# A ring of eight weight columns, and the low part of new expert weights ahead of the low part of the rows, in a mixture-of-experts stage

## Chip, core and metric

The kernel runs on one NeuronCore of a Trainium2 chip. The metric is the device time of one execution in microseconds (us). Its engines are TensorE (PE in the profile, PEld its weight loads), VectorE (DVE), ScalarE (ACT), GpSimd (POOL) and SyncE (SP). Each takes its instructions in order from a sequencer of its own, which also does the register work, the branches and the waits (a q behind the engine's name); semaphores order the engines among each other.

## The reference

Two residual layers on x of 4 x 2048 x 512 floats: a small selective state space model, and then a mixture of 64 experts, which is the part in question:

```python
swb = sigmoid(einsum('bsd,de->bse', x, w_router)) + b_router
...                                    # 4 of 8 groups, then 8 of 64 experts for each token
topk_w = 2.5 * topk_w / sum(topk_w)
sort = argsort(idx_flat); tok = sort // 8; x_sorted = x_flat[tok]
g = ragged_dot(x_sorted, we_gate, group_sizes)      # 512 -> 256, of each row's expert
u = ragged_dot(x_sorted, we_up, group_sizes)        # 512 -> 256
o = ragged_dot(silu(g) * u, we_down, group_sizes)   # 256 -> 512
y = zeros.at[tok].add(o * w_sorted[:, None])
```

There are 8192 tokens with 8 experts each, and a shared expert besides, which an earlier stage does.

## The kernel before

Earlier stages normalize, scan the states, route the tokens and write a table: 576 tiles of 128 rows, each of one expert. The last stage, `expert_tiles`, goes through that table; it is all that the change touches. One word of the table (`Words`, read by `value_load` at L1301) holds a tile's expert, the slot of its weights, and whether the expert is new, so that its weights have to be made. 64 of the tiles are such.

fp32 products are made of rounded parts: a factor's high part is its cast to float32r, its low part the difference to it; a product is high times high, high times low, and low times high. So each step has these pieces, i being the tile:

- `turn_x(i)` (TensorE, L1407): four transposes of the gathered rows into `ps_x`, the one buffer that there is of it.
- `keep_x(i)` (ScalarE): the high part of `ps_x` (`xT_high`, L1524), then the row numbers (L1526) and the column of routing weights (`weight`, L1528).
- `keep_low(i)` (VectorE, L1587): the low part of `ps_x` (`xT_low`). Only after it may `ps_x` be written again: `turn_x(i + 1)` waits for `xT_low_ready`.
- `split_high(i, part)` (ScalarE, L1516) and `split_low(i, part)` (VectorE, L1579): the high and low part of a new expert's weights, part 0 for gate and up (128 x 2048), part 1 for down (128 x 1024). For other tiles the engine only looks at the word, branches past, drains and counts the semaphore up ("the look").
- `gate_up(i)` (TensorE, L1437): twelve matmuls, eight with `xT_high`, four with `xT_low`. It waits for `w_low_ready[0]`, which `split_low(i, 0)` counts up. Between its matmuls TensorE's sequencer reads ahead words of the table (`read_ahead`): up to three, by the tile's place in a cycle of eight; in tiles that are multiples of eight one more stands ahead of it (L1487).
- `activate` (ScalarE, silu, L1535), `hidden` (VectorE, product, L1599), `turn_h`, `keep_h`, `keep_h_low`, `down` (TensorE, L1456), and `scale(i)` (VectorE, L1606): output rows times `weight`, in `y`. GpSimd adds them to the output and gathers rows ahead.
- Every four tiles VectorE marks (`mark`, L1611) and picks (`pick`, L1618 to L1627) which rows belong to tiles to come, and TensorE searches between (`find`, L1419): mark in VectorE's steps with i%4 = 2, find in TensorE's with i%4 = 3.

The orders are written by hand in each engine's `step(i, s)`. TensorE: `turn_x(i + 1)`, `find` in every fourth step, `gate_up(i)`, `turn_h(i - 1)`, `down(i - 2)`. VectorE: `keep_low(i + 1)`, `split_low(i + 1, 0)`, `split_low(i, 1)`, pick or mark, `hidden(i)`, `keep_h_low(i - 1)`, `scale(i - 2)`. ScalarE: row numbers, `keep_x(i + 1)`, `split_high(i + 2, 0)`, `split_high(i + 1, 1)`, `activate(i)`, `keep_h(i - 1)`. So a new tile n has the first half of its weights made low in VectorE's step n - 1, while TensorE works on tile n - 1, and the second half in step n. `weight` has four columns; `keep_x(i)` writes one of them after `scale(i - 4)` has read it.

Of the kernel before, what the change touches and what calls it, by code (L numbers as in the profile page):

```python
# [5 lines left out]
ALU = mybir.AluOpType  # L6
# [8 lines left out]
P = 128  # L15
# [18 lines left out]
UNROLL, SHORT = 8, 4  # L34
# [7 lines left out]
def after(eng, sem, count):  # L42

    if not isinstance(count, int) or count > 0:
        eng.wait_ge(sem, count)
# [1152 lines left out]
def expert_tiles(nc, k):  # L1198
# [8 lines left out]
    with ExitStack() as ctx:  # L1207
        def sb(name, shape, dt=F32):
            return ctx.enter_context(nc.sbuf_tensor("e_" + name, shape, dt))
# [12 lines left out]
        x_ids = sb("x_ids", [P, UNROLL], U32)  # L1222
        y_ids = sb("y_ids", [P, UNROLL], U32)
        x = sb("x", [P, XS, ROW])
        weight = sb("weight", [P, SHORT])
        xT_high = sb("xT_high", [P, 2, DC, P], F32R)
        xT_low = sb("xT_low", [P, 2, DC, P], F32R)
        silu = sb("silu", [P, 2, F])
# [41 lines left out]
        y_made = sem("y_made")  # L1270
# [26 lines left out]
        def exists(i):  # L1297
            return not isinstance(i, int) or 0 <= i < TILES
# [206 lines left out]
        @block.scalar  # L1505
        def _(act):
            words = Words(act)

            def split_high(i, s, part):
                if part == 0:  # L1510
                    act.wait_ge(w_loaded[s % WS], 48 // WS * (i - s % WS) + 48)
                    after(act, gu_done, i - WSLOTS + 1)
                else:
                    after(act, y_done, i - WSLOTS + 1)
                act.sem_inc(act_begun, 1)
                split_weights(act, words, s, lambda half, place: nc.scalar.copy(  # L1516
                    w_high[:, bass.ds(place, 1), PARTS[part]], w_raw[:, bass.ds(half, 1), PARTS[part]]))
                act.drain().then_inc(w_high_ready[part], 1)  # L1518

            def keep_x(i, s, slot):  # L1520
                e = act.snap(words.expert(s), min_val=0, max_val=E - 1)
                act.wait_ge(xt_done, i + 1)
                after(act, gu_done, i - 1)
                nc.scalar.copy(xT_high[:, s % 2], ps_x[:]).then_inc(xT_high_ready, 1)  # L1524
                after(act, retired, i - YS + 2)
                nc.scalar.copy(y_ids[:, bass.ds(slot, 1)], tile_ids[:, bass.ds(i, 1)])  # L1526
                after(act, y_made, i - SHORT + 1)
                nc.scalar.copy(weight[:, s % SHORT:s % SHORT + 1],  # L1528
                               x[:, bass.ds(slot, 1), bass.ds(e + D, 1)].rearrange("p o d -> p (o d)")) \
                    .then_inc(weight_ready, 1)  # L1530

            def activate(i, s):
                act.wait_ge(gu_done, i + 1)
                after(act, h_made, i - 1)
                nc.scalar.activation(silu[:, s % 2, :], ps_gu[s % 2][:, 0, :], ACT.Silu).then_inc(silu_ready, 1)  # L1535

            def keep_h(i, s):
                act.wait_ge(ht_done, i + 1)
                after(act, y_done, i - 1)
                nc.scalar.copy(hT_high[:, s % 2], ps_h[:]).then_inc(hT_high_ready, 1)  # L1540

            def take_ids(i, column):
                act.wait_ge(picked, i + 1)
                nc.scalar.copy(x_ids[:, bass.ds(column, 1)], tile_ids[:, bass.ds(i, 1)]).then_inc(ids_ready, 1)  # L1544

            def step(i, s, slot):
                if s == 0:
                    words.load(i + 1, s + 1)
                words.load(i + 2, (s + 2) % SHORT)
                if exists(i + AHEAD_IDS):  # L1550
                    take_ids(i + AHEAD_IDS, slot(AHEAD_IDS))
                if exists(i + 1):
                    keep_x(i + 1, (s + 1) % SHORT, slot(1))
                if exists(i + 2):
                    split_high(i + 2, (s + 2) % SHORT, 0)
                if exists(i + 1):
                    split_high(i + 1, (s + 1) % SHORT, 1)
                activate(i, s)
                if exists(i - 1):
                    keep_h(i - 1, (s - 1) % SHORT)  # L1560

            for i in range(AHEAD_IDS):
                take_ids(i, i)
            for i in range(2):
                words.load(i, i)
                split_high(i, i, 0)
            split_high(0, 0, 1)
            keep_x(0, 0, 0)
            short_walk(act, step)
            keep_h(TILES - 1, SHORT - 1)  # L1570

        @block.vector
        def _(v):
            words = Words(v)

            def split_low(i, s, part):
                v.wait_ge(w_high_ready[part], i + 1)
                v.sem_inc(dve_begun, 1)
                split_weights(v, words, s, lambda half, place: nc.vector.tensor_tensor(  # L1579
                    w_low[:, bass.ds(place, 1), PARTS[part]], w_raw[:, bass.ds(half, 1), PARTS[part]],  # L1580
                    w_high[:, bass.ds(place, 1), PARTS[part]].bitcast(F32), ALU.subtract))
                v.drain().then_inc(w_low_ready[part], 1)

            def keep_low(i, s):
                v.wait_ge(xT_high_ready, i + 1)
                after(v, gu_done, i - 1)
                nc.vector.tensor_tensor(xT_low[:, s % 2], ps_x[:], xT_high[:, s % 2].bitcast(F32),  # L1587
                                        ALU.subtract).then_inc(xT_low_ready, 1)
# [13 lines left out]
            def scale(i, s, slot):  # L1602
                v.wait_ge(y_done, i + 1)
                v.wait_ge(weight_ready, i + 1)
                after(v, retired, i - YS + 2)
                nc.vector.tensor_scalar(y[:, bass.ds(slot, 1), :].rearrange("p o d -> p (o d)"), ps_y[s % 2][:],  # L1606
                                        weight[:, s % SHORT:s % SHORT + 1], None, ALU.mult).then_inc(y_made, 1)

            def mark(i):

# [19 lines left out]
            def step(i, s, slot):  # L1630
                if s == 0:
                    words.load(i, s)
                words.load(i + 1, (s + 1) % SHORT)
                if exists(i + 1):
                    keep_low(i + 1, (s + 1) % SHORT)
                    split_low(i + 1, (s + 1) % SHORT, 0)
                split_low(i, s, 1)
                if s == 1 and exists(i - s - SHORT + AHEAD_FIND):
                    pick(i - s - SHORT + AHEAD_FIND, 2)
                if s == 2 and exists(i - s + AHEAD_FIND):  # L1640
                    mark(i - s + AHEAD_FIND)
                if s == 3 and exists(i - s + AHEAD_FIND):
                    pick(i - s + AHEAD_FIND, 0)
                hidden(i, s)
                if exists(i - 1):
                    keep_h_low(i - 1, (s - 1) % SHORT)
                if exists(i - 2):
                    scale(i - 2, (s - 2) % SHORT, slot(UNROLL - 2))
# [100 lines left out]
```

## Time and profile before

| | before |
|---|---|
| median of 3 runs (lowest to highest) | 3974.49 us (3974.14 to 3979.03) |
| the profiled execution | 3973.47 us, span 3971.7 us |
| busy: TensorE, VectorE, ScalarE, GpSimd | 92%, 58%, 34%, 40% of the span |
| granted TensorE clock, mean | 0.971 of full speed |

`expert_tiles` is the part from about 900 us to the end. The timeline lists instructions by start in us from the start of the span, with their duration, engine, line, operation, tiles, how many were merged, and in brackets how long the engine had been idle before, and what ended it. TensorE's ends are modelled, and its instructions overlap. Steps are therefore measured from start to start.

### The profile page before, as it was taken

How to read it: one execution, taken by the hardware profiler on the slowest of the kernel's cores; microseconds unless marked ns; L12 is line 12 of the kernel's file. 1: busy time of each engine (PE TensorE's matmuls, PEld its weight loads, DVE VectorE, ACT ScalarE, POOL GpSimd, SP SyncE). 2: the span in 40 equal slices, each digit the busy share in tenths (PEclk: the TensorE clock that was granted, in tenths of full speed). 3: DMA queues.
4: the chain of work that ended last, by engine and by line, in shares of the span. 5: the costliest groups of instructions: out<-in, count | busy, mean ns of one | idle time of the engine just before them, and what ended most of it. 6: DMA issues, size and time to landing. Idle time of an engine off the chain costs nothing.

```text
span 3971.7 us, 110141 instructions
## 1 busy us (share of the span) xinstructions
PE 3650.4 (92%) x16856; PEld 2774.8 (70%) x16857; DVE 2313.6 (58%) x5802; ACT 1349.9 (34%) x4031; POOL 1602.0 (40%) x1208
## 2 busy tenths in 40 slices
PE   6809999967999999999999999999999999999996
PEld 3404445536877777787778778787888777787785
DVE  5364555555666665656665565656555666666653
ACT  2212222213333433434333343334333343334331
POOL 1010000004555555555555455555555555455443
PEclk9959999988999999999999999999999999999998
DMA  3322323225666676667666666666666676666654
GB/s 113 106 61 86 98 97 98 96 56 122 125 154 149 153 155 122 149 127 167 141 134 127 158 137 124 138 139 152 124 127 140 122 169 153 140 133 154 137 102 74
DMA packets 216177, 502.40 MB, mean 126 GB/s; under 512 B 46587, under 2 KB 46715, under 8 KB 215360
## 3 DMA queue, kind: packets, MB, share of 16 engines
q0 software_dynamic: 129024, 320.94, 43.4%
q1 hardware_dynamic: 86592, 177.77, 13.6%
q10 hardware_dynamic: 512, 3.15, 0.3%
q8 instruction: 17, 0.28, 0.0%
q14 instruction: 32, 0.26, 0.0%
HBM read 1115.65 MB, written 191.41 MB: 329 GB/s over the span
## 4 chain that ended last, share of the span: by engine, by line
PE 59%; DVE 5%; issue 5%; DVEq 2%; ACT 2%; DMA 2%; ACTq 1%; POOLq 0%; POOL 0%; SPq 0%
PE e_ps_gu L1437 34%; PE e_ps_y L1456 16%; PE e_ps_x L1407 5%; DVE e_w_low L1579 3%; PE e_ps_h L1466 3%; ACT e_w_high L1516 2%; DMA out<-e_y,e_y_ids 2%; PE e_ps_find L1419 1%; DVEq L1301 1%; ACTq L1301 1%; DVE e_past L1611 1%; DVE e_y L1606 1%; DVE e_below L1622 0%; DVEq L1579 0%; ACT e_silu L1535 0%
## 5 line engine op out<-in xcount | busy, mean ns | idle before, releaser
L1381 POOL DMA_INDIRECT out<-e_y,e_y_ids x576 | 935.9, 1625 | 1326.5 <-ACT e_weight L1528 582.4
L1373 POOL DMA_INDIRECT e_x<-token_rows,e_x_ids x576 | 615.9, 1069 | 273.5 <-issue 172.7
L1437 PE MATMUL e_ps_gu<-e_w_high,e_xT_high 128*128 x2304 | 688.4, 419 | 15.1 <-issue 5.1
L1437 PE MATMUL e_ps_gu<-e_w_low,e_xT_high 128*128 x2304 | 646.6, 399 | 6.4 <-issue 4.8
L1437 PE MATMUL e_ps_gu<-e_w_high,e_xT_low 128*128 x2304 | 650.4, 401 | 0.2 <-issue 0.2
L1606 DVE TENSOR_SCALAR e_y<-e_ps_y,e_weight 128x512 f32 (+1 forms) x576 | 430.9, 748 | 243.6 <-PE e_ps_y L1456 202.9
L1587 DVE TENSOR_TENSOR e_xT_low<-e_ps_x,e_xT_high 128x512 fp32r<-128x512 f32 x576 | 397.7, 690 | 286.9 <-ACT e_xT_high L1524 173.6
L1437 PEld LDWEIGHTS e_ps_gu<-e_w_high,e_xT_low 128*128 128x128 f32 x2304 | 428.8, 189 | 128.1 <-issue 29.2
L1437 PEld LDWEIGHTS e_ps_gu<-e_w_low,e_xT_high 128*128 128x128 f32 x2304 | 428.8, 188 | 126.5 <-issue 31.1
L1535 ACT ACTIVATE e_silu<-e_ps_gu 128x256 f32<-128x256 f32 x576 | 221.2, 384 | 821.5 <-PE e_ps_gu L1437 627.0
L1437 PEld LDWEIGHTS e_ps_gu<-e_w_high,e_xT_high 128*128 128x128 f32 x2304 | 396.2, 191 | 98.1 <-issue 37.3
L1524 ACT CAST e_xT_high<-e_ps_x 128x512 fp32r<-128x512 f32 x576 | 336.5, 584 | 294.1 <-PE e_ps_x L1407 289.2
L1456 PE MATMUL e_ps_y<-e_w_high,e_hT_high 128*128 x1152 | 411.6, 438 | 0.0
L1407 PEld LDWEIGHTS e_ps_x<-ident,e_x 128*128 128x128 f32 x2304 | 366.5, 204 | 57.2 <-issue 6.5
L1599 DVE TENSOR_TENSOR e_h<-e_silu,e_ps_gu 128x256 f32<-128x256 f32 x576 | 241.6, 419 | 282.2 <-ACT e_silu L1535 259.8
L1407 PE MATMUL e_ps_x<-ident,e_x 128*128 128x128 f32 x2304 | 365.7, 281 | 7.8 <-DVE e_xT_low L1587 6.8
L1456 PE MATMUL e_ps_y<-e_w_high,e_hT_low 128*128 x1152 | 362.5, 396 | 0.0
L1456 PE MATMUL e_ps_y<-e_w_low,e_hT_high 128*128 x1152 | 362.5, 396 | 0.0
L1544 ACT CAST e_x_ids<-e_tile_ids (+1 forms) x576 | 110.1, 192 | 503.6 <-issue 403.5
L1466 PEld LDWEIGHTS e_ps_h<-ident,e_h 128*128 128x128 f32 x1152 | 226.4, 197 | 51.7 <-DVE e_h L1599 3.4
L1456 PEld LDWEIGHTS e_ps_y<-e_w_high,e_hT_low 128*128 128x128 f32 x1152 | 218.2, 189 | 51.1
L1579 DVE TENSOR_TENSOR e_w_low<-e_w_raw,e_w_high x128 | 225.4, 1761 | 48.7 <-ACTq L1518 25.0
(245 smaller groups left out, 3926.0 us busy)
## 6 DMA issues: line engine op xcount, KB each, us to landing
e_w_raw<-in_L_ffn_we_gate SPq DMA_DIRECT2D x576, 512.0 KB
e_w_raw<-in_L_ffn_we_up SPq DMA_DIRECT2D x576, 512.0 KB
e_w_raw<-in_L_ffn_we_down SPq DMA_DIRECT2D x576, 512.0 KB
a_x<-in_L_attn_x SPq DMA_DIRECT2D x64, 256.0 KB, 3.4
t_x_in<-in_L_attn_x SPq DMA_DIRECT2D x64, 256.0 KB, 2.8
token_rows<-t_xn SPq DMA_DIRECT2D x64, 256.0 KB, 3.1
out<-t_y_out SPq DMA_DIRECT2D x64, 256.0 KB, 2.0
e_x<-token_rows,e_x_ids POOLq DMA_INDIRECT x576
```

Source lines behind the costliest of these rows:

```text
L1373: pool.indirect_dma_start(x[:, s % XS, :], None, k.rows, bass.IndirectOffsetOnAxis(x_ids[:, s:s + 1], 0)) \
L1381: pool.indirect_dma_start(k.out, bass.IndirectOffsetOnAxis(y_ids[:, s:s + 1], 0), y[:, s % YS, :], None, compute_op=ALU.add).then_inc(adde ...
L1407: last = nc.tensor.transpose(ps_x[:, c, :], chunks[:, c, :], k.ident[:])
L1437: last = nc.tensor.matmul(ps_gu[s % 2][:], x[:, s % 2, c, :], w[:, c], start=(n == 0), stop=(n == 3 * DC - 1))
L1456: last = nc.tensor.matmul(ps_y[s % 2][:], x[:, s % 2, c, :], w[:, c], start=(n == 0), stop=(n == 3 * FC - 1))
L1466: last = nc.tensor.transpose(ps_h[:, c, :], chunks[:, c, :], k.ident[:])
L1524: nc.scalar.copy(xT_high[:, s % 2], ps_x[:]).then_inc(xT_high_ready, 1)
L1535: nc.scalar.activation(silu[:, s % 2, :], ps_gu[s % 2][:, 0, :], ACT.Silu).then_inc(silu_ready, 1)
L1579: split_weights(v, words, s, lambda half, place: nc.vector.tensor_tensor(w_low[:, bass.ds(place, 1), PARTS[part]], w_raw[:, bass.ds(half, ...
L1587: nc.vector.tensor_tensor(xT_low[:, s % 2], ps_x[:], xT_high[:, s % 2].bitcast(F32), ALU.subtract).then_inc(xT_low_ready, 1)
L1599: nc.vector.tensor_tensor(h[:, s % 2, :], silu[:, s % 2, :], ps_gu[s % 2][:, 1, :], ALU.mult).then_inc(h_made, 1)
L1606: nc.vector.tensor_scalar(y[:, bass.ds(slot, 1), :].rearrange("p o d -> p (o d)"), ps_y[s % 2][:], weight[:, s % SHORT:s % SHORT + 1], Non ...
```

## The change

The ring `weight` gets eight columns in place of four, so that `keep_x(i)` waits for `scale(i - 8)`; the column is found by a register in place of a constant. And VectorE does `split_low(i + 1, 0)` ahead of `keep_low(i + 1)`.

```diff
-        weight = sb("weight", [P, SHORT])
+        weight = sb("weight", [P, UNROLL])
...
-                after(act, y_made, i - SHORT + 1)
-                nc.scalar.copy(weight[:, s % SHORT:s % SHORT + 1],
+                after(act, y_made, i - UNROLL + 1)
+                nc.scalar.copy(weight[:, bass.ds(slot, 1)],
...
-                                        weight[:, s % SHORT:s % SHORT + 1], None, ALU.mult).then_inc(y_made, 1)
+                                        weight[:, bass.ds(slot, 1)], None, ALU.mult).then_inc(y_made, 1)
...
                 if exists(i + 1):
+                    split_low(i + 1, (s + 1) % SHORT, 0)
                     keep_low(i + 1, (s + 1) % SHORT)
-                    split_low(i + 1, (s + 1) % SHORT, 0)
                 split_low(i, s, 1)
```

What it moves stands in VectorE's order, here from the read of the table word to the branch for the down part, in the step with the mark. Names start with e_; "waits" are the semaphores that a row waits for. Before:

```order
L1301 TENSOR_LOAD tiles
L1301 ISA x2
L1585 REGISTER_ALU
L1587 TENSOR_TENSOR e_xT_low<-e_ps_x,e_xT_high 128x512 [waits e_gu_done,e_xT_high_ready]
L1328 REGISTER_ALU [waits e_w_high_ready0]
L1328 COMPARE_AND_BRANCH
L1579 REGISTER_ALU x2
L1579 ISA
L1579 REGISTER_ALU
L1579 TENSOR_TENSOR e_w_low<-e_w_raw,e_w_high 128x2048
L1328 UNCONDITIONAL_BRANCH
L1328 COMPARE_AND_BRANCH [waits e_w_high_ready1]
```

The same place in the changed kernel:

```order
L1301 TENSOR_LOAD tiles
L1301 ISA x2
L1577 REGISTER_ALU
L1328 REGISTER_ALU [waits e_w_high_ready0]
L1328 COMPARE_AND_BRANCH
L1579 REGISTER_ALU x2
L1579 ISA
L1579 REGISTER_ALU
L1579 TENSOR_TENSOR e_w_low<-e_w_raw,e_w_high 128x2048
L1328 UNCONDITIONAL_BRANCH
L1587 TENSOR_TENSOR e_xT_low<-e_ps_x,e_xT_high 128x512 [waits e_gu_done,e_xT_high_ready]
L1328 COMPARE_AND_BRANCH [waits e_w_high_ready1]
```

The low part of the rows (L1587) has moved behind the low part of the weights and behind the register work and branch ahead of that; the branch for the down part now follows it directly.

TensorE's order is the same in both kernels. This is where it waits for the two, behind the transposes of h of one step; the rows are the last ones of a step and the first ones of the next:

```order
L1466 MATMUL e_ps_h<-ident,e_h 128x128 [waits e_h_made]
L1466 MATMUL e_ps_h<-ident,e_h 128x128
L1407 MATMUL e_ps_x<-ident,e_x 128x128 [waits e_xT_low_ready,e_gathered3]
L1407 MATMUL e_ps_x<-ident,e_x 128x128 x3
L1437 REGISTER_ALU [waits e_h_made,e_xT_high_ready,e_w_low_ready0]
L1437 ISA
L1437 MATMUL e_ps_gu<-e_w_high,e_xT_high 128x512
```

The wait for the rows' low part stands ahead of the four transposes, the wait for the weights' low part behind them; both rows have kept their places.

## Rows read from the trace of the kernel before

**Rows 1.** Page, part 4: the chain that ended last, shares by line.
```profile
PE e_ps_gu L1437 34%; PE e_ps_y L1456 16%; PE e_ps_x L1407 5%; DVE e_w_low L1579 3%; PE e_ps_h L1466 3%; ACT e_w_high L1516 2%; DMA out<-e_y,e_y_ids 2%; PE e_ps_find L1419 1%; DVEq L1301 1%; ACTq L1301 1%; DVE e_past L1611 1%; DVE e_y L1606 1%; DVE e_below L1622 0%; DVEq L1579 0%; ACT e_silu L1535 0%
```

**Rows 2.** Timeline of TensorE, a step with no new expert.
```profile
2919.46 0.63 PE L1407 MATMUL e_ps_x<-ident,e_x 128*128 128x128 f32 x4
2919.85 1.17 PE L1437 MATMUL e_ps_gu<-e_w_high,e_xT_high 128*128 x4
...
2921.79 1.10 PE L1437 MATMUL e_ps_gu<-e_w_high,e_xT_low 128*128 x4
...
2924.37 0.63 PE L1407 MATMUL e_ps_x<-ident,e_x 128*128 128x128 f32 x4
```

**Rows 3.** Page, part 5: groups of VectorE; count, busy us, mean ns, idle before.
```profile
L1587 DVE TENSOR_TENSOR e_xT_low<-e_ps_x,e_xT_high 128x512 fp32r<-128x512 f32 x576 | 397.7, 690 | 286.9 <-ACT e_xT_high L1524 173.6
...
L1579 DVE TENSOR_TENSOR e_w_low<-e_w_raw,e_w_high x128 | 225.4, 1761 | 48.7 <-ACTq L1518 25.0
```

**Rows 4.** Timeline of VectorE in its step 384; tile 385 is new.
```profile
2932.26 0.69 DVE L1587 TENSOR_TENSOR e_xT_low<-e_ps_x,e_xT_high 128x512 fp32r<-128x512 f32 x1 [1.27 <-ACT e_xT_high L1524]
2932.93 2.29 DVE L1579 TENSOR_TENSOR e_w_low<-e_w_raw,e_w_high  x1
```

**Rows 5.** Timeline of TensorE, its step 385.
```profile
2934.73 0.63 PE L1407 MATMUL e_ps_x<-ident,e_x 128*128 128x128 f32 x4
2935.49 0.96 PE L1437 MATMUL e_ps_gu<-e_w_high,e_xT_high 128*128 x3
...
2938.33 1.31 PE L1437 MATMUL e_ps_gu<-e_w_high,e_xT_low 128*128 x4
...
2941.11 0.63 PE L1407 MATMUL e_ps_x<-ident,e_x 128*128 128x128 f32 x4
```

**Rows 6.** TensorE's sequencer in that time: duration ns min/median/max, first and last start.
```profile
L45 PEldq EVENT_SEMAPHORE  x1: 51/51/51, 2933.0 to 2933.0; - x1
...
L1437 PEldq ALU_OP  x1: 36/36/36, 2935.3 to 2935.3; - x1
...
L1301 PEldq TENSOR_LOAD <-tiles x3: 299/302/307, 2935.9 to 2938.0; - x3
```

**Rows 7.** Timeline of VectorE in its step 414; tile 414 is new.
```profile
3090.36 0.72 DVE L1611 TENSOR_TENSOR e_past<-slot_row,begin 64x512 bf16<-64x512 f32 x1 [0.21 <-issue]
```

**Rows 8.** Timeline of TensorE, the start of its step 415.
```profile
3090.18 0.63 PE L1407 MATMUL e_ps_x<-ident,e_x 128*128 128x128 f32 x4
3091.27 0.73 PE L1419 MATMUL e_ps_find<-ranks,e_past 64*128 x4 [0.45 <-DVE e_past L1611]
```

**Rows 9.** Timeline of ScalarE in its step 321; tile 323 is new.
```profile
2606.28 0.19 ACT L1528 COPY e_weight<-e_x 128x1 f32 x1 [0.34 <-DVE e_y L1606]
2606.80 1.91 ACT L1516 CAST e_w_high<-e_w_raw  x1 [0.32 <-issue]
```

**Rows 10.** Timeline of VectorE, from the end of its step 321 into 322.
```profile
2610.30 0.74 DVE L1606 TENSOR_SCALAR e_y<-e_ps_y,e_weight 128x512 f32 x1
2611.43 0.69 DVE L1587 TENSOR_TENSOR e_xT_low<-e_ps_x,e_xT_high 128x512 fp32r<-128x512 f32 x1 [0.39 <-ACT e_xT_high L1524]
2612.08 2.29 DVE L1579 TENSOR_TENSOR e_w_low<-e_w_raw,e_w_high  x1
2614.98 0.68 DVE L1611 TENSOR_TENSOR e_past<-slot_row,begin 64x512 bf16<-64x512 f32 x1 [0.61 <-issue]
```

**Rows 11.** Timeline of TensorE, in its step 323.
```profile
2615.86 0.72 PE L1419 MATMUL e_ps_find<-ranks,e_past 64*128 x4 [0.81 <-DVE e_past L1611]
```

**Rows 12.** Timeline of VectorE in its steps 239 and 240; tile 240 is new.
```profile
2166.83 2.31 DVE L1579 TENSOR_TENSOR e_w_low<-e_w_raw,e_w_high  x1
...
2173.41 0.69 DVE L1587 TENSOR_TENSOR e_xT_low<-e_ps_x,e_xT_high 128x512 fp32r<-128x512 f32 x1 [1.03 <-issue]
```

**Rows 13.** Waits: who, for whom; us in total, times, longest.
```profile
ACT e_weight L1528 <- DVE e_y L1606: 210.5, 237, 3.2
...
PE e_ps_x L1407 <- DVE e_xT_low L1587: 6.8, 3, 6.1
```

## The prediction

> **What bounds the kernel now.** I read the page's chain of work that ended last first: 55% of it is TensorE's gate/up, down and transposing matmuls (34 + 16 + 5), 3% VectorE's low part of new weights (L1579) [rows 1]. Then the timeline of TensorE where nothing new is loaded. From one block of four transposes (L1407) to the next a step takes 2924.37 - 2919.46 = 4.91 us; gate/up starts 0.39 after the transposes and lasts to 2921.79 + 1.10, 3.04 us [rows 2]. No row there has idle time ahead of it, so a plain step can gain nothing. What can be won or lost lies at new experts: L1579 has 128 instructions [rows 3], two per new expert, so 64 tiles bring new weights; the first opens the stage, 63 stand in it. For those I read VectorE's, ScalarE's and TensorE's timelines around one tile of each kind. The kind is the tile's place in VectorE's cycle of four steps, because the search work differs by step. Placing the 128 instructions among the 576 of L1587 gives 10 tiles n with n%4 = 1, 18 with 2, 17 with 3 and 18 with 0, of which 8 are multiples of 8.
>
> The reader is to see what ends TensorE's wait there. For tile 385 VectorE does keep_low at 2932.26 (0.69 long, done 2932.95) and then the low part, 2932.93 + 2.29 = 2935.22 [rows 4]. TensorE's transposes of the next tile start at 2934.73 with no wait, gate/up of 385 at 2935.49; the step is 2941.11 - 2934.73 = 6.38, 1.47 over a plain one [rows 5]. Little of this is the wait for the low part itself: gate/up lasts to 2938.33 + 1.31 = 2939.64, 4.15 us instead of 3.04. The sequencer's rows show why. It passes a wait (L45) at 2933.0, just as keep_low ends and 1.7 before those transposes run; it stands at gate/up until 2935.3, just after the low part; and only then reads three words of the tile table, from 2935.9 to 2938.0, in between issuing matmuls [rows 6]. So **TensorE's sequencer is held by keep_low ahead of the transposes and by the low part ahead of gate/up, and after the last release gate/up ends 2939.64 - 2935.22 = 4.42 us later.** At the transposes themselves TensorE hardly ever waits for keep_low today: 6.8 us in three times [rows 13].
>
> **The change, part by part.** *The swap.* It adds no data work: 64 low parts and 576 keep_lows stay. Before, keep_low came first and released the transposes while the low part ran. Now the low part comes first, so keep_low ends about 2.3 us later at every new expert, and TensorE's transposes, which stand ahead of gate/up in its program, wait for both in turn.
>
> Tile 385: the low part can start where keep_low did, 2932.26, plus the sequencer's look at the table word, the branch and the addresses, which was hidden under keep_low and took at most 0.67 (2932.93 - 2932.26). Bounds 2932.26 and 2932.93; I take 2932.75, near the upper, since VectorE was waiting on its sequencer there. It ends 2935.04. keep_low follows after a drain and two waits: between 0 and the 0.69 of a skipped part; I take 0.2, then 0.69: 2935.93. The transposes, at 2934.73 before, start at about 2936.0. The sequencer is released at 2935.98 instead of 2935.22, issues four transposes (0.2) and then has the same 4.42: gate/up ends at 2940.6 instead of 2939.64. **+1.0 us.** Nine tiles of this kind; the tenth, 257, follows two other new experts within three tiles, so that other waits may cover it, and I count it 0: **+9.0**.
>
> n%4 = 2 (tile 414): the same +1.0 in its own step, but the next step has the search, and that waits today: its transposes start at 3090.18, the search only at 3091.27, after the mark (L1611) at 3090.36 + 0.72 [rows 7, 8]. TensorE being 1.0 later at 3091.2 + 0.6 finds the mark about done. VectorE's own way to the mark hardly changes: in the step of the low part the look at the down part now hides under keep_low, but the look at the gate/up part comes bare. **+0.1, 18 tiles: +1.8**, bounds -0.2 and +0.5.
>
> n%4 = 3 (tile 323): here the mark is in the same step as the low part, and the search waits for it until 2615.86 [rows 10, 11]; the transposes are early in any case. VectorE waited for ScalarE before keep_low (0.39), and the low part started at 2612.08 [rows 10]. *The ring* acts here: ScalarE's copy of the weight column waited 0.34 for VectorE's scaling of four tiles back [rows 9], and behind it on ScalarE stand the 1.91 us high part of the new expert, the silu, and with it VectorE's product and scaling. Without that wait all of it moves up by about 0.35; in all, ScalarE gives 210.5 us to this wait [rows 13], nearly all of it where nothing hangs on it. With the swap the low part starts no sooner than the scaling's end (2610.30 + 0.74 = 2611.04) and no later than the look's 0.67 behind keep_low's old start (2612.10), both less 0.35; I take 2611.35, between the two, 0.7 earlier. keep_low (0.2 + 0.69) now stands between it and the mark, but hides some 0.55 of the 0.61 from the low part's end (2614.37) to the mark (2614.98). 0.7 - 0.9 + 0.55 = 0.35: **-0.35, 17 tiles: -6.0**, bounds 0 and -0.75.
>
> n%4 = 0 (tile 240): the low part ends at 2166.83 + 2.31 = 2169.14; half a us earlier with ring and swap, but then keep_low (0.2 + 0.69) follows, and the sequencer is released at 2169.55, 0.37 later than now [rows 12]. At multiples of 8 one more table word is read between transposes and gate/up (L1487), so far behind the wait's cover: bounds 0.3, a bare load, and 1.05, the spacing of the three [rows 6]; I take 0.7. With 0.2 for the transposes 1.27, of which I take 0.9, because the next step waits for a late keep_low today (1.03 idle ahead of it [rows 12]) and then no longer does: **8 tiles, +7.2**. The other 10 have slack in their own step (the step before has the search), but in the next keep_low comes some 0.3 later through the bare look: **+0.3, 10 tiles: +3.0**.
>
> *Elsewhere.* The ring's register column adds one register instruction to ScalarE; in plain steps both have idle time. In a plain step keep_low comes later by the look without new weights: between 0 and 0.67, I take 0.4. The tightest place is the one of tile 385's L45 row: the sequencer is released 1.7 ahead of the transposes, then 1.3. Issuing gate/up with its three words took from 2935.3 to 2938.0 and some 0.7 for the last word, 3.4 us for 3.04 of matmuls, so about 0.9 is left over, and I count 0. If that cover is gone it is the third rival.
>
> Sum: 9.0 + 1.8 - 6.0 + 7.2 + 3.0 = **+15.0 us**. The profiled execution took 3973.47; so 3988.5 there, and against the median of 3974.49, which is 1.0 above it, **3989**.
>
> [...] The sequencer's rows [rows 6] show it stopped at the wait ahead of the transposes until keep_low is done, as its next instruction, the one at gate/up, comes only after. [...]
>
> **The rivals.** (1) *The sequencer isn't held at the transposes.* Then it reads its words under the wait, gate/up follows the transposes by 0.39 and lasts 3.04 [rows 2]: tile 385 ends at 2939.4 (-0.2 x 10 = -2), 414 goes by the mark (-0.2 x 18 = -3.6), 323 as above (-6), and n%4 = 0 loses today's stall of the next step (about 0.5, half of its 1.03, x 18 = -9): -20.6, **3954**, faster. For it: every low part does come earlier. Against: the sequencer's rows [rows 6]. It decides if gate/up ends within 3.5 us of keep_low's end. Chance 0.15. (2) *Gains and losses cancel*: the look costs nothing on VectorE and tile 323's kind gains 0.75 (-13), while 385's loses 0.7 (+6) and the rest as above at half: within 8 us of **3974**. Chance 0.27. (3) *Plain steps lose too*: if that 0.9 isn't there, for table words that come slowly, 0.2 in each of some 138 steps with i%4 = 1 adds 28: **4017**. Against: the slack, and steps that run without idle time now [rows 2]. Chance 0.1. That the change doesn't do what it says, a swap without effect since VectorE's sequencer is the limit, is the lower bound of tile 385's shift and lies in (2).
>
> **How the numbers follow.** My forecast has 0.48, with its own range 3978 to 4002 from the bounds. A measurement of this kernel tells about 0.2%, 8 us, from no change. Faster: rival 1 and a part of 2, 0.18. Same: most of 2 and the low end of the forecast, 0.26. Slower: the rest, 0.56. The range 3956 to 4008 leaves out the far halves of 1 and 3.
>
> **What would show it.** Right: in the profile after, L1407 waits on e_xT_low L1587 about 1 us at the tiles with n%4 = 1 and 2, some 25 to 30 us in all, where now it is 6.8 [rows 13]; ScalarE's wait of e_weight on e_y is gone; the search's wait on e_past is smaller. Wrong: no wait at L1407, or gate/up after it in 3.05 us, or plain steps over 4.91.

## The result, and the profile after

| | before | changed |
|---|---|---|
| median of 4 runs each (lowest to highest) | 3976.28 us (3974.14 to 3979.03) | 4046.31 us (4041.55 to 4050.68) |
| ratio to before | | 1.0175, 95% interval 1.0158 to 1.0193 |
| span of the profiled execution | 3971.7 us | 4046.0 us |
| granted TensorE clock, mean | 0.971 | 0.969 |

The changed kernel is 70 us slower, where 15 was forecast and the third rival said 43. The chain that ended last has gained TensorE, VectorE's share of new weights (L1579) stays at 3% [rows 1]:

```profile
PE e_ps_gu L1437 37%; PE e_ps_y L1456 17%; PE e_ps_x L1407 6%; DVE e_w_low L1579 3%; PE e_ps_h L1466 3%; PE e_ps_find L1419 1%; DMA out<-e_y,e_y_ids 1%; ACT e_w_high L1516 1%; DVEq L1301 1%; DVE e_xT_low L1587 1%; DMA e_w_raw<-in_L_ffn_we_down 0%; DVEq L1579 0%; DVE e_past L1611 0%; ACTq L1301 0%; ACT e_silu L1535 0%
```

The waits that the prediction named have changed as it said; ScalarE's wait of `weight` for the scaling no longer stands in the list [rows 13]. In the changed kernel:

```profile
PE e_ps_x L1407 <- DVE e_xT_low L1587: 37.5, 34, 5.8
...
PE e_ps_find L1419 <- DVE e_past L1611: 8.5, 18, 2.7
```

The second of the two stood in the kernel before as

```profile
PE e_ps_find L1419 <- DVE e_past L1611: 29.5, 34, 2.7
```

At the transposes there are 37.5 us in 34 waits, where 25 to 30 were forecast and 6.8 in 3 stood before. So the waits at new experts came as expected; what they cost is told further down. Tile 385 once more, VectorE, then TensorE [rows 4, 5], then the L45 row of TensorE's sequencer, its next wait behind those transposes [rows 6]:

```profile
2988.99 2.29 DVE L1579 TENSOR_TENSOR e_w_low<-e_w_raw,e_w_high  x1 [1.83 <-issue]
2991.48 0.69 DVE L1587 TENSOR_TENSOR e_xT_low<-e_ps_x,e_xT_high 128x512 fp32r<-128x512 f32 x1 [0.20 <-issue]
```

```profile
2992.23 0.75 PE L1407 MATMUL e_ps_x<-ident,e_x 128*128 128x128 f32 x4 [1.19 <-DVE e_xT_low L1587]
...
2995.37 1.30 PE L1437 MATMUL e_ps_gu<-e_w_high,e_xT_low 128*128 x4
...
2998.14 0.63 PE L1407 MATMUL e_ps_x<-ident,e_x 128*128 128x128 f32 x4
```

```profile
L45 PEldq EVENT_SEMAPHORE  x1: 51/51/51, 2992.2 to 2992.2; - x1
```

keep_low starts 0.20 after the low part, as taken. The transposes wait 1.19 for it (1.27 forecast). The sequencer passes L45 at 2992.2, and gate/up ends at 2995.37 + 1.30 = 2996.67, 4.50 behind keep_low's end at 2992.17 (forecast: 2940.6 - 2935.93 = 4.67).

What was not forecast stands where nothing new is loaded. A step's length is taken from one block of transposes to the next. Of the 338 steps that are neither n - 1, n, n + 1 nor n + 2 of a new expert, those with i%4 = 1 rose from 4.91 to 5.37 (medians; 86 steps, +31.1 us in sum), those with i%8 = 2 from 4.91 to 5.09 (42 steps, +5.0); the medians of all others, sorted by i%8, kept their length to 0.01. Step 365 of the changed kernel, TensorE:

```profile
2886.09 0.63 PE L1407 MATMUL e_ps_x<-ident,e_x 128*128 128x128 f32 x4
2886.47 1.17 PE L1437 MATMUL e_ps_gu<-e_w_high,e_xT_high 128*128 x4
2887.48 1.34 PE L1437 MATMUL e_ps_gu<-e_w_low,e_xT_high 128*128 x4
2888.66 1.31 PE L1437 MATMUL e_ps_gu<-e_w_high,e_xT_low 128*128 x4
```

The blocks of four follow each other at 1.01 and 1.18 us, and the last two last 1.34 and 1.31 instead of 1.10 [rows 2]: TensorE is given its matmuls late. What stands behind that is told by the step ahead of it. In the kernel before, the timeline has the transposes that open step 364, GpSimd's add (L1381), and VectorE's keep_low:

```profile
2828.38 0.63 PE L1407 MATMUL e_ps_x<-ident,e_x 128*128 128x128 f32 x4
...
2830.42 1.59 POOL L1381 DMA_INDIRECT out<-e_y,e_y_ids  x1 [2.58 <-ACT e_x_ids L1544]
...
2830.81 0.69 DVE L1587 TENSOR_TENSOR e_xT_low<-e_ps_x,e_xT_high 128x512 fp32r<-128x512 f32 x1 [1.27 <-ACT e_xT_high L1524]
```

and the sequencer's groups, the same wait (L45) behind step 365's transposes, and TensorE's next read of a table word, the first of three for step 365 (ns minimum/median/maximum, first and last start):

```profile
L45 PEldq EVENT_SEMAPHORE  x1: 51/51/51, 2831.6 to 2831.6; - x1
L1301 PEldq TENSOR_LOAD <-tiles x1: 307/307/307, 2832.2 to 2832.2; - x1
```

The same rows of the changed kernel, timeline, wait and read:

```profile
2881.17 0.63 PE L1407 MATMUL e_ps_x<-ident,e_x 128*128 128x128 f32 x4
...
2883.24 1.59 POOL L1381 DMA_INDIRECT out<-e_y,e_y_ids  x1 [2.57 <-ACT e_x_ids L1544]
...
2884.14 0.69 DVE L1587 TENSOR_TENSOR e_xT_low<-e_ps_x,e_xT_high 128x512 fp32r<-128x512 f32 x1 [1.77 <-issue]
```

```profile
L45 PEldq EVENT_SEMAPHORE  x1: 51/51/51, 2884.9 to 2884.9; - x1
L1301 PEldq TENSOR_LOAD <-tiles x1: 972/972/972, 2885.6 to 2885.6; - x1
```

So keep_low starts 2.43 and 2.97 into the step, 0.54 later; the sequencer passes its wait 1.7 and 1.2 ahead of the transposes (2833.29 and 2886.09); the read starts 3.9 and 4.4 into the step, 0.5 later; the add 2.04 and 2.07, nearly unchanged. And the read, which took 0.31, takes **0.97**. The two together, 0.52 (median of keep_low's shift in such steps) and 0.66, are 1.18, of which the step lost 0.46. The rest, 0.72, was covered: so far the sequencer could fall back before TensorE had to wait for it.

### The profile page after: what moved, and what is told of

Same layout as the page of the kernel before. It is cut to its first block, busy times and chain, and to the rows that moved or that the text cites. A ratio compares the mean times of both kernels' runs of the same rounds, so it can differ in the third digit from the quotient of the medians.

```text
span 4046.0 us, 110981 instructions
## 1 busy us (share of the span) xinstructions
PE 3709.8 (92%) x16856; PEld 2751.2 (68%) x16857; DVE 2324.6 (57%) x5802; ACT 1312.1 (32%) x4031; POOL 1670.9 (41%) x1208
## 4 chain that ended last, share of the span: by engine, by line
PE 64%; DVE 4%; issue 3%; DVEq 2%; DMA 2%; ACT 1%; ACTq 1%; SPq 0%; POOLq 0%; POOL 0%
PE e_ps_gu L1437 37%; PE e_ps_y L1456 17%; PE e_ps_x L1407 6%; DVE e_w_low L1579 3%; PE e_ps_h L1466 3%; PE e_ps_find L1419 1%; DMA out<-e_y,e_y_ids 1%; ACT e_w_high L1516 1%; DVEq L1301 1%; DVE e_xT_low L1587 1%; DMA e_w_raw<-in_L_ffn_we_down 0%; DVEq L1579 0%; DVE e_past L1611 0%; ACTq L1301 0%; ACT e_silu L1535 0%
## 5 line engine op out<-in xcount | busy, mean ns | idle before, releaser
L1381 POOL DMA_INDIRECT out<-e_y,e_y_ids x576 | 1016.5, 1765 | 1326.2 <-SPq L1351 673.3
L1373 POOL DMA_INDIRECT e_x<-token_rows,e_x_ids x576 | 604.3, 1049 | 272.8 <-issue 174.7
L1587 DVE TENSOR_TENSOR e_xT_low<-e_ps_x,e_xT_high 128x512 fp32r<-128x512 f32 x576 | 398.5, 692 | 496.2 <-ACTq L1518 259.1
L1437 PE MATMUL e_ps_gu<-e_w_low,e_xT_high 128*128 x2304 | 669.2, 402 | 12.1 <-issue 9.1
L1437 PE MATMUL e_ps_gu<-e_w_high,e_xT_low 128*128 x2304 | 674.7, 405 | 0.5 <-issue 0.5
L1437 PEld LDWEIGHTS e_ps_gu<-e_w_low,e_xT_high 128*128 128x128 f32 x2304 | 420.0, 188 | 163.3 <-issue 78.1
L1437 PEld LDWEIGHTS e_ps_gu<-e_w_high,e_xT_low 128*128 128x128 f32 x2304 | 418.7, 189 | 161.9 <-issue 73.7
L1407 PE MATMUL e_ps_x<-ident,e_x 128*128 128x128 f32 x2304 | 371.3, 283 | 38.8 <-DVE e_xT_low L1587 37.5
L1579 DVE TENSOR_TENSOR e_w_low<-e_w_raw,e_w_high x128 | 225.1, 1759 | 61.2 <-issue 32.9
L676 POOL TENSOR_TENSOR t_rstd<-t_var_eps,nhalf 128x4 f32<-128x4 f32 x16 | 16.1, 1008 | 575.0 <-DVE t_var_eps L896 575.0
```

Of the source, the lines that this page charges most:

```text
L1373: pool.indirect_dma_start(x[:, s % XS, :], None, k.rows, bass.IndirectOffsetOnAxis(x_ids[:, s:s + 1], 0)) \
L1381: pool.indirect_dma_start(k.out, bass.IndirectOffsetOnAxis(y_ids[:, s:s + 1], 0), y[:, s % YS, :], None, compute_op=ALU.add).then_inc(adde ...
L1407: last = nc.tensor.transpose(ps_x[:, c, :], chunks[:, c, :], k.ident[:])
L1437: last = nc.tensor.matmul(ps_gu[s % 2][:], x[:, s % 2, c, :], w[:, c], start=(n == 0), stop=(n == 3 * DC - 1))
```

## The experiments

In all of them a step counts as plain when it is none of n - 1 to n + 2 of a new expert; step lengths, read times and their places are medians over such steps. The earlier stages end between 907 and 917 us in these profiles, which has nothing to do with the edits; the step lengths are free of it. The first question was which half of the change costs, and by which way. Theory A: the later release of TensorE's sequencer together with a read that has become slow. Theory B: the later release alone. Theory C: the swapped order itself.

**The ring alone** (e1_ring): the two lines of the swap put back, the ring of eight kept.

> The ring of eight alone, VectorE's order as before. All theories agree that the loss comes from the swap: about 3968 us (3960 to 3974). Tiles with n%4 = 3 gain some 0.4 us each (17 tiles, -7); steps with i%4 = 1 away from new experts stay at 4.91; reads of table words on TensorE over 0.5 us as many as before (193), not 284. If instead the plain steps' loss came from the ring (ScalarE's earlier copies), they would stand at 5.36 here and the time at 4010 or more.

3970.39 us (3964.37 to 3979.35), ratio 0.998 (0.997 to 0.999). Steps n of the 17 tiles with n%4 = 3 gained 0.37 each, plain steps stayed at 4.91, and TensorE's reads over 0.5 us are no more than before (189; 201 before, 295 in the changed kernel). The ring is not the loss. By the medians it is worth 8 us, where 7 were said; the steps of the profiled execution don't bear that out, as the 6.3 us at n%4 = 3 stand against 5.2 lost in steps n at n%4 = 2, and in all they are 1.6 shorter.

**The swap alone** (e2_swap): `weight` with four columns as before.

> The swap alone, the ring of four kept. If the two parts add up: the changed kernel's 4046 plus the 7 us that the ring gave, about 4053 us (4044 to 4062); steps with i%4 = 1 at about 5.36, as in the changed kernel. If ring and swap help each other at tiles with n%4 = 3, the swap alone costs more than that, over 4062.

4039.43 us (4037.89 to 4047.01), ratio 1.0158 (1.0138 to 1.0179); plain steps with i%4 = 1 at 5.33. The loss is the swap's. The parts don't add up, the other way from what was feared: the ring gives nothing beside the swap, as tiles with n%4 = 3 gain 0.46 by the swap alone and 0.55 by both. (Of the 7 us between this run and the changed kernel, 1.2 lie in the steps of this stage.)

**Only late** (e4_look): the ring of eight, the old order, and an empty look ahead of keep_low.

```diff
                 if exists(i + 1):
+                    v.sem_inc(dve_begun, 1)
+                    with v.If(words.is_new((s + 1) % SHORT)):
+                        v.drain()
+                    v.drain()
                     keep_low(i + 1, (s + 1) % SHORT)
                     split_low(i + 1, (s + 1) % SHORT, 0)
```

> The ring of eight with the old order, and an empty look (semaphore, word, branch, drain, no data) ahead of the low part of the rows: only the lateness of that low part in plain steps, about 0.5 us, without the swap. Theories A and B: plain steps with i%4 = 1 cost 5.3 to 5.4 as in the changed kernel, some 100 steps x 0.4, and new experts up to 0.5 each: 4015 to 4050 us. Theory C (it is the swapped order itself, the rows' low part behind the weights' low part, that costs): plain steps stay at 4.91, time within 15 us of the ring alone.

4027.81 us (4025.40 to 4035.06), ratio 1.0129 (1.0108 to 1.0149): 57 us over the ring alone, with no data moved and no order changed. keep_low ends 0.39 later than with the ring alone, and plain steps with i%4 = 1 stand at 5.24, a little under the 5.3 that was expected. The first read of step 365 on the sequencer, and the transposes at the step's two ends:

```profile
L1301 PEldq TENSOR_LOAD <-tiles x1: 926/926/926, 2864.6 to 2864.6; - x1
```

```profile
2865.22 0.63 PE L1407 MATMUL e_ps_x<-ident,e_x 128*128 128x128 f32 x4
...
2870.43 0.63 PE L1407 MATMUL e_ps_x<-ident,e_x 128*128 128x128 f32 x4
```

2870.43 - 2865.22 = 5.21. Theory C is out: the lateness of keep_low by the look is enough to make plain steps longer, and the read is slow with it. (By the steps, 24 of the 55 us lost against the ring alone lie in plain steps, the others near new experts.)

**The gather moved** (e3_gather). Slow reads stood next to GpSimd's gathers (L1373), so the gather of GpSimd's step 4 was issued right behind that of step 3.

```diff
-                if exists(i + AHEAD_X):
+                if s != 4 and exists(i + AHEAD_X):
                     gather(i + AHEAD_X, (s + AHEAD_X) % UNROLL)
+                if s == 3 and exists(i + 1 + AHEAD_X):
+                    gather(i + 1 + AHEAD_X, (s + 1 + AHEAD_X) % UNROLL)
```

> The changed kernel with GpSimd's gather of its step 4 (of 8) issued one step earlier, right behind the gather of step 3. Theory A (TensorE's sequencer is released 0.5 us later AND its first table word then falls behind the start of a gather, where it takes 0.95 us in place of 0.30; there is about 0.7 us of slack): plain steps with i%8 = 5 fall from 5.37 to about 4.91, those with i%8 = 1, which are not touched, stay at 5.36; the long reads at the end of step 4 go; about 4026 us (4018 to 4036). Theory B (the later release alone costs it, the slack is under 0.1 us): i%8 = 5 stays at 5.3 to 5.4, time 4046 +- 5.

4048.44 us (4048.03 to 4052.58), ratio 1.0178 (1.0159 to 1.0196). i%8 = 5 stayed at 5.41, i%8 = 1 at 5.31. By the numbers that was theory B's result, but the rows around step 365 say something else: the read, then the timeline of GpSimd and TensorE (whose transposes are L1409 in this kernel):

```profile
L1301 PEldq TENSOR_LOAD <-tiles x1: 1027/1027/1027, 2887.4 to 2887.4; - x1
```

```profile
2882.80 0.98 POOL L1373 DMA_INDIRECT e_x<-token_rows,e_x_ids  x1 [0.30 <-issue]
2885.08 1.61 POOL L1381 DMA_INDIRECT out<-e_y,e_y_ids  x1 [1.30 <-SPq L1351]
...
2887.92 0.63 PE L1409 MATMUL e_ps_x<-ident,e_x 128*128 128x128 f32 x4
...
2893.34 0.39 PE L1409 MATMUL e_ps_x<-ident,e_x 128*128 128x128 f32 x2
```

The gather is gone from the place, the add is not, and the read still takes 1.03. So the gather was the wrong partner; it had only stood 0.3 us behind an add each time. Sorted by the time since the end of the last add, TensorE's reads between 1000 and 3900 us give:

| start of the read after the end of an add, us | before: reads, median us, over 0.5 us | changed: reads, median us, over 0.5 us |
|---|---|---|
| 0 to 0.15 | 26, 0.31, none | 23, 0.30, none |
| 0.15 to 0.5 | 188, 0.35, 19 | 90, 0.30, 18 |
| 0.5 to 0.9 | 121, 0.93, 118 | 215, 0.93, 205 |
| 0.9 to 1.35 | 67, 0.60, 51 | 89, 0.56, 56 |
| 1.35 to 1.75 | 188, 0.31, 8 | 34, 0.31, 2 |
| over 1.75 | 653, 0.30, none | 764, 0.30, 2 |

Most of the slow ones end together, 1.71 us after the add's end (median), whenever they began: reads stand still from about 0.4 to 1.7 us after an add has been issued. The same holds for the reads of VectorE and ScalarE (medians 0.95 and 0.84 at 0.5 to 0.9, 0.31 and 0.28 from 1.75 on, in the kernel before). For step 365 this is 2884.83 + 0.4 to 2884.83 + 1.7 = 2885.2 to 2886.5 in the changed kernel, into which a read at 2885.6 falls; before, 2832.01 + 0.4 = 2832.4 is just behind the read that began at 2832.2. Theory A2: the add is the partner.

**The add held back behind the next gather** (e5_add).

```diff
-                if exists(i - 2):
-                    add(i - 2, (s - 2) % UNROLL)
+                for back in {3: (), 4: (3, 2)}.get(s, (2,)):
+                    if exists(i - back):
+                        add(i - back, (s - back) % UNROLL)
```

> The changed kernel with GpSimd's accumulating output transfer (L1381, the add) of its step 3 of 8 held back behind the gather of step 4. Theory A2, which takes the gather's place after its move changed nothing: the reads of table words on every engine stand still from about 2.0 to 3.3 us after the start of an add, which at plain steps with i%8 = 0 and 4 is 4.05 to 5.35 us into TensorE's step; a first read that starts at 4.4 ends at 5.37, one at 3.9 has passed. With the add of step 4 moved away, plain steps with i%8 = 5 fall from 5.38 to 4.91 to 4.97 and their first read takes 0.31; those with i%8 = 1, whose add stays, remain at 5.37; about 4027 us (4018 to 4036). Theory B (the 0.5 us of later release alone, whatever the reads do): i%8 = 5 stays over 5.3 and the time at 4046 +- 5.

4045.26 us (4041.50 to 4049.47), ratio 1.0172 (1.0152 to 1.0192), i%8 = 5 at 5.41. The edit did not do what it was meant to: with no add ahead of it the gather of step 4 went up to where it is in the kernel before this one, and the add stayed at 2.07 into the step. It repeats that experiment and decides nothing more.

**The add really moved** (e9_add): one add in eight waits for the next tile's rows too.

```diff
-                pool.wait_ge(y_made, i + 1)
+                pool.wait_ge(y_made, i + 1 + (s == 1))
```

> The changed kernel with one add in eight really moved: GpSimd's add of tiles with i%8 = 1 waits for the next tile's output rows as well, so it starts one TensorE step later. (Holding it behind the next gather had only let that gather go earlier; the add stayed at 2.07.) Theory A2 (reads of table words stand still 2.0 to 3.3 us after an add's start): in plain steps with i%8 = 5 the first read, at 4.40, takes 0.31 and not 0.97, and the step falls from 5.38 to 4.91 to 4.97; i%8 = 1 stays at 5.37. The adds behind it come later too, so a few steps with i%8 = 6 or 7 may lose up to 0.3. Time 4028 us (4018 to 4042). Theory B (release alone): i%8 = 5 stays over 5.3.

The first read of step 365; then the timeline, the last add ahead of the read and the transposes at the step's two ends:

```profile
L1301 PEldq TENSOR_LOAD <-tiles x1: 307/307/307, 2905.9 to 2905.9; - x1
```

```profile
2898.12 1.59 POOL L1381 DMA_INDIRECT out<-e_y,e_y_ids  x1 [2.17 <-SPq L1351]
...
2906.42 0.63 PE L1407 MATMUL e_ps_x<-ident,e_x 128*128 128x128 f32 x4
...
2911.34 0.63 PE L1407 MATMUL e_ps_x<-ident,e_x 128*128 128x128 f32 x4
```

The read, 4.40 into the step as in the changed kernel, takes 0.31; plain steps with i%8 = 5 are back at 4.91, those with i%8 = 1, whose add was left, stand at 5.29. keep_low ends at 3.66 as late as in the changed kernel, so **the release alone costs nothing, and theory B falls**. The changed kernel's own trace says the same with nothing moved: of its 86 plain steps with i%4 = 1, in all of which keep_low ends at about 3.65, the 64 whose first read took over 0.8 us have a median of 5.37, the 10 whose read took under 0.4 one of 4.91. The time is 4085.34 us (4077.80 to 4090.66), ratio 1.0275 (1.0254 to 1.0295), against an expected 4028: plain steps gave back 15.1 us, but steps near new experts lost 48.7. There ScalarE now waits 61.5 us in 17 times for new weights to arrive (1.6 us, once, in the changed kernel; SyncE starts their loads behind its wait for the adds, `retire`), and 18 gate/ups ran in part at a granted clock of 0.50, 3 in the changed kernel. How the 48.7 divide was not worked out. As a version it is worse, as a test it is clear.

**The read moved** (e6_word): in the changed kernel, the first of a step's words is read ahead of the transposes.

```diff
             def step(i, s):
+                read_ahead(i, s, 0)
                 if exists(i + 1):
                     turn_x(i + 1, (s + 1) % UNROLL)
...
-                        if n in (3, 6, 9):
+                        if n in (6, 9):
                             read_ahead(i, s, n // 3 - 1)
```

> The changed kernel with the first of the up to three table words of a TensorE step read ahead of the transposes, so ahead of the wait for the rows' low part, instead of behind gate/up's third matmul. Theory A2: what costs is a read behind the late release, not the release itself. Plain steps with i%4 = 1 fall from 5.37 to 4.91 to 5.0 (some 45 us in all), new experts with n%4 = 1 and 2 lose one word behind the release (28 x 0.5 to 0.75): about 3985 us (3970 to 4002). Theory B (the later release as such): steps stay over 5.2, time over 4030.

3980.45 us (3973.55 to 3985.00), ratio 0.9996 (0.9979 to 1.0012): the same kernel as before within the interval, with ring and swap in it. The plain steps of the kinds that had risen are at 4.91 again; step 365:

```profile
2842.45 0.63 PE L1407 MATMUL e_ps_x<-ident,e_x 128*128 128x128 f32 x4
...
2847.36 0.39 PE L1407 MATMUL e_ps_x<-ident,e_x 128*128 128x128 f32 x2
```

One read a step, moved in front of the late release, gives back 66 of the 70 us: 38.6 in plain steps, 27.2 near new experts. By itself this run can't tell a slow read behind the release from any read there; the run before it can.

**The same read in the old order** (e7_ring_word): ring of eight, and the edit just shown.

> Ring of eight, old order, and the first table word read ahead of the transposes. If the 4.4 us from the last release to the end of gate/up at new experts is made of table words (A2), the 28 tiles with n%4 = 1 and 2 gain 0.5 to 0.75 each, tiles that are multiples of 8 up to 0.7: 3970 - 14 to - 26 = 3944 to 3956 us, plain steps still 4.91. If gate/up is held by something else there: 3970 +- 4.

3972.69 us (3969.41 to 3980.22), ratio 0.9989 (0.9979 to 0.9999); against the ring alone no gain. The gain at new experts did come (step n: -0.73 at n%4 = 1, -0.69 at n%4 = 2), and at n%4 = 2 the next step took 1.40 back. TensorE in step 303 (302 is new), and the same stretch by windows (sum of time, then busy us of each engine, then the granted clock):

```profile
2511.97 0.63 PE L1407 MATMUL e_ps_x<-ident,e_x 128*128 128x128 f32 x4
2513.82 0.73 PE L1419 MATMUL e_ps_find<-ranks,e_past 64*128 x4 [1.22 <-DVE e_past L1612]
2514.66 1.21 PE L1437 MATMUL e_ps_gu<-e_w_high,e_xT_high 128*128 x4
2515.70 1.89 PE L1437 MATMUL e_ps_gu<-e_w_low,e_xT_high 128*128 x4
```

```profile
2511.97:2513.77 1.80, 0.63 (x5) 0.44 (x3) 1.59 (x3) 0.77 (x3) 1.50 (x2) 1.00 0.47 35
...
2515.77:2518.97 3.20, 3.20 (x9) 2.43 (x8) 0.95 (x6) 0.00 (x0) 2.58 (x2) 0.50 0.52 91
```

The search now waits 1.22 us for VectorE's mark, where it waited 0.43 in this step before; in step 415 it is 1.22 instead of 0.45 [rows 8]. What TensorE gained it gave to the next wait. And behind that wait the granted clock was 0.50 of full speed for the 3.2 us shown, in which four matmuls took 1.89 and not 1.10. In this kernel 11 gate/ups have that clock in part of their time, the stage's very first and 10 in steps with the search; in the kernel before they are 3, the first among them and one in a step with the search. In plain steps with i%4 = 1 the first read behind the release is now the second word; it starts at 4.29 and takes 0.92, yet with keep_low done at 3.17 the step stays at 4.91. So a slow read alone costs nothing there either.

**Two words early** (e8_ring_words): the second word too, ahead of gate/up's wait for the low part.

> As the one before, and the second word read ahead of gate/up's wait for the weights' low part. Two effects against each other, both of A2: at new experts another 0.3 to 0.7 us for 45 to 60 tiles (-15 to -40); in plain steps the second read comes at about 3.6 to 4.2 us into the step, close to the standstill from 4.05 on: if it falls into it, gate/up starts up to 0.4 us late in up to half of the steps (+50 to +100). Clean of that: about 3930 us (3920 to 3945); with it: 3980 to 4040, and the plain steps then show 5.1 to 5.4 in their first matmuls' wait.

4014.18 us (4009.47 to 4025.97), ratio 1.01 (1.0075 to 1.0126). The time lies in the range given for the bad case, the reason does not: plain steps stayed at 4.91. The loss is in steps with the search behind a new expert (against the ring alone +2.39 at n%4 = 2, in step n + 1, +1.37 at n%4 = 3, in step n, and +0.72 at n%4 = 1, in step n + 2), where gate/up follows a late mark, and 22 gate/ups have a granted clock of 0.50 in part of their time.

**The mark earlier** (e11_ring_mark, ring of eight and old order; e10_ring_word_mark, with the read ahead of the transposes as well): VectorE marks at the end of its step s = 1, behind the scaling, not in step s = 2.

```diff
-                if s == 2 and exists(i - s + AHEAD_FIND):
-                    mark(i - s + AHEAD_FIND)
...
                     scale(i - 2, (s - 2) % SHORT, slot(UNROLL - 2))
+                if s == 1 and exists(i - s + AHEAD_FIND):
+                    mark(i - s + AHEAD_FIND)
```

> Ring of eight, old order, and the earlier mark alone (no word moved). The mark alone is worth the excess of about 1.0 in steps n+1 of the 18 tiles with n%4 = 2 and part of the 1.1 left at n%4 = 3: 3970 - 20 to - 35 = 3935 to 3950 us; less than the run with both by 10 to 20 us.

> Ring of eight, old order, first table word ahead of the transposes, and VectorE's mark at the end of the step before, behind the scaling, instead of behind the weights' low part. If what the earlier word gained at n%4 = 2 was given back in the next step to the search, which waits for the mark: steps n+1 of these 18 tiles lose their excess of over 1 us, and n%4 = 3 another 0.3 to 0.8: 3973 - 25 to - 50 = 3923 to 3948 us. If the search is held by something else: 3973 +- 5.

The mark alone: 3940.47 us (3931.02 to 3946.66), ratio 0.9907 (0.9881 to 0.9932). With the read: **3921.99 us** (3920.07 to 3925.03), ratio 0.9862 (0.9844 to 0.9880), 56 us faster than before and just under the range given. The mark now ends long ahead of the search of step 415 (414 is new), which waits for nothing:

```profile
3051.78 0.67 DVE L1612 TENSOR_TENSOR e_past<-slot_row,begin 64x512 bf16<-64x512 f32 x1
...
3053.69 0.63 PE L1407 MATMUL e_ps_x<-ident,e_x 128*128 128x128 f32 x4
3054.26 0.40 PE L1419 MATMUL e_ps_find<-ranks,e_past 64*128 x4
```

Against the kernel with the read alone, steps n + 1 at n%4 = 2 fell by 2.45 and steps n at n%4 = 3 by 1.49; one gate/up has a granted clock of 0.50 in part of its time, the very first.

**The swap with both helps** (e12_word_mark): the changed kernel with the read and the mark moved.

> The changed kernel (ring and swap) with the word ahead of the transposes and the earlier mark: the same two helps as the run with the old order, so the difference of the two is what the swap costs once neither the plain steps' reads nor the mark are in the way. By my forecast's terms that is +1.0 at n%4 = 1 and 2 and +0.3 to 0.9 at n%4 = 0: 25 to 45 us above the old order with both, about 3970 us (3955 to 3985). If the swap were harmless by then: within 8 us of it.

3964.07 us (3960.14 to 3968.45), ratio 0.9965 (0.9953 to 0.9978): 42 us above the old order with the same two edits. By the steps all of it lies near new experts (+45.9, and -0.6 in plain ones): at n%4 = 1 +1.40 in step n - 1 and -0.47 in step n, 0.93 where the forecast's first term said 1.0, and at n%4 = 2 +1.48 and -0.21, as no late mark covers it now.

## Why the prediction was wrong

**The step that failed** is the sentence on plain steps: "so about 0.9 is left over, and I count 0". It had three sizes in it, and plain steps lost 36.4 us of the 69.6 by which all steps together rose. keep_low is 0.52 later in a plain step, where 0.4 was taken. The cover, 1.7 - (3.4 - 3.04) = 1.3 by the prediction's numbers and 0.9 behind its shift of 0.4, was 0.72. And a read was taken to cost the 0.30 of [rows 6] wherever it stands; shifted by half a us it falls behind the end of an add and takes 0.97. 0.52 + 0.66 - 0.72 = 0.46 in each step with i%4 = 1. The shift alone would have cost nothing, as the run with the add moved shows, and with a cover of 1.3 shift and slow read together would have cost nothing either: it took the cover and the read both.

The 0.72 comes out of this same sum, so it is no check on it. The run with the empty look gives a second figure, 0.39 + 0.63 - 0.33 = 0.69, and step 365 of the kernel before a third, by its three reads and gate/up's last four matmuls:

```profile
L1301 PEldq TENSOR_LOAD <-tiles x3: 295/307/350, 2832.2 to 2834.4; - x3
```

```profile
2835.63 1.10 PE L1437 MATMUL e_ps_gu<-e_w_high,e_xT_low 128*128 x4
```

The third word is read behind the ninth of the twelve matmuls. With the prediction's 0.7 for a word it is done at about 2835.1, and the tenth matmul, the second of the four, runs from about 2835.63 + 0.23 (a quarter of the 0.94 from block to block): some 0.7 us of cover, an estimate. The prediction had set the words' 3.4 us against the whole 3.04 of gate/up, though three matmuls stand behind the last word.

The third rival had the right steps and the right engine, "for table words that come slowly". That its 28 us come near the 31.1 that steps with i%4 = 1 lost is luck: it took 0.2 in some 138 steps, and it was 0.46 in 86.

**The new experts** lost 33.2 us where 15.0 were forecast, so they hold 18 us of the miss. Summed over steps n - 1 to n + 2 the four kinds lost, forecast beside it: n%4 = 1 9.7 (9.0), n%4 = 2 9.5 (1.8), n%4 = 3 2.6 (-6.0), n%4 = 0 20.2 (10.2). (Where tiles stand close together a step is counted twice, so the four don't add up to the total.) The 43 new tiles with no other new one within three give, per tile, 0.85 at n%4 = 1 (forecast 1.0), 0.28 at n%4 = 2 (0.1), and 0.14 at n%4 = 3 (-0.35). The mechanism of the first two holds: at n%4 = 2 step n - 1 lost 1.5, and step n + 1, with the search, gave 0.97 back. At n%4 = 3 the tile's own step gained the 0.35, but step n - 1 lost 0.22 and step n + 2, which has i%4 = 1, 0.27, for which the forecast had nothing. At n%4 = 0 multiples of 8 lost 1.49 each (0.9) and the ten others 0.83 (0.3); how much of that is slow reads, no run separates. Of the terms for single tiles, keep_low's gap of 0.2 and the wait of 1.2 at the transposes stand in the rows of tile 385, where steps 384 and 385 together grew by 0.91 (1.0 forecast); the 0.2 in it for issuing four transposes was the author's estimate, which no run shows by itself, and the stretch that it is part of, from keep_low's end to gate/up's, was 4.50 where 4.67 was forecast; 0.37 by the ring at n%4 = 3 was forecast as 0.35.

**The first rival**, that the sequencer isn't held at the transposes, falls. The transposes of tile 385 waited 1.19 us, and gate/up still ended 4.50 after keep_low, where the rival was to show in an end within 3.5. No word was read under that wait: in the changed kernel the sequencer's group for this tile is

```profile
L1301 PEldq TENSOR_LOAD <-tiles x3: 299/302/307, 2993.0 to 2995.1; - x3
```

so all three reads start behind keep_low's end at 2992.17. The L45 row says the same. It is not the wait for keep_low itself but the next one behind the transposes, and it starts at 2933.0, 2831.6, 2884.9 and 2992.2 in the four places shown, within 0.1 us of keep_low's ends at 2932.95, 2831.50, 2884.83 and 2992.17. The second rival is out by the time.

## What to carry to other kernels

A step that is only moved, without more work, can cost as much as the work around it, if what it releases is a sequencer that reads words of a table, as here, where the reads behind it took 0.31 or 0.97 us by their distance to an add: look not only at how much later the release comes, but at what the reads behind it then run into. Before counting a delay as covered, work the cover out from the rows of a plain step, at the matmul behind the last read and not at the end of the block, and add up all that shifts with it, and price it for every step, not only for those that the change is about: 0.46 us in each of some 86 plain steps, 31 us in sum, came to as much as all 63 new experts, 33 us. And ask at which wait an engine will spend what it gains at another: with the ring and the old order the early read gave nothing, as TensorE waited 1.22 us for the mark in place of 0.43 and 0.45, and with the early mark the three gave 1.4%.

## What the hardware showed

- In the kernel before, reads of table words stood still, on every sequencer with enough of them to tell, from about 0.4 to 1.7 us after GpSimd's accumulating add had been issued: those that began 0.5 to 0.9 us behind it had medians of 0.93 us on TensorE, 0.95 on VectorE, 0.84 on ScalarE and 0.82 on SyncE (37 reads), where TensorE's from 1.75 on had 0.30. The gather without an add near it did not do this: in the kernel with the gather moved, 299 of TensorE's reads began within 1.35 us of a gather's end and over 1.75 behind the last add, with a median of 0.30 and 2 over 0.5. What in the add's transfer holds them was not tried, and stays open.
- After 1.2 us without work at the wait for the mark, the granted clock of TensorE was 0.50 for the 3.2 us shown in step 303 of the kernel with the ring and the early read, and stayed at 1.00 in its step 415, with the same wait (idle 1.22). What tells them apart stays open.
